# Two engines instead of one copy the transposed activations out of PSUM in a fused layernorm and linear kernel on eight cores

## The reference

```python
def reference(L0_attn_x, L0_ffn_weight, L0_ffn_bias, L0_ffn_kk, L0_ffn_aa):   # x: (1, 8192, 4096) f32
    def _L0_attn_ref(x):
        b, c, l = x.shape                       # b is 1
        q = jnp.transpose(x, (2, 0, 1))
        scale = jnp.asarray(c, x.dtype) ** 0.5
        scores = jnp.einsum('lnc,lmc->lnm', q, q) / scale
        prob = jax.nn.softmax(scores, axis=-1)
        msg = jnp.einsum('lnm,lmc->lnc', prob, q)
        return x + jnp.transpose(msg, (1, 2, 0))
    def _L0_ffn_ref(x, weight, bias, kk, aa):   # weight: (4096, 4096)
        w_b = aa * jnp.tanh(kk * weight)
        y = jnp.einsum('bsi,oi->bso', x, w_b)
        return y + bias
    x = L0_attn_x
    x = x + _L0_attn_ref(_layernorm(x, axis=-1))
    x = x + _L0_ffn_ref(_layernorm(x, axis=-1), L0_ffn_weight, L0_ffn_bias, L0_ffn_kk, L0_ffn_aa)
    return x
```

## Time and profile before

| | |
|---|---|
| median of 2 runs | 607.36 us (606.45 and 608.27) |
| the profiled execution | 604.37 us |
| its span on the slowest core, core 5 | 602.8 us |
| spans of the other cores | 592.7 to 600.9 us |
| TensorE busy | 498.2 us (83%) |
| ScalarE busy | 216.7 us (36%) |
| VectorE busy | 150.3 us (25%) |
| GpSimd busy | 83.6 us (14%) |

### The profile page before, as it was taken

One profiled execution on the slowest core, in us unless ns is written; L12 is line 12 of the kernel. 1 busy time (PEld: TensorE's weight loads), 2 busy tenths in 40 slices (PEclk: granted clock), 3 DMA queues, 4 the chain that ended last, 5 costly groups with the idle time before them and its releaser, 6 DMA issues.

```text
span 602.8 us, 7078 instructions; the slowest of 8 cores (592.7 to 602.8 us)
## 1 busy us (share of the span) xinstructions
PE 498.2 (83%) x2379; PEld 231.4 (38%) x2379; DVE 150.3 (25%) x336; ACT 216.7 (36%) x228; POOL 83.6 (14%) x118
## 2 busy tenths in 40 slices
PE   3034577556388999999999999998999899999993
PEld 3021133223244444444444444443444344444441
DVE  0800335632782120311032003200220023031120
ACT  0256577665544363036203722361036105500000
POOL 0001000020001120203030303030303031221111
PEclk9555676788598999999999999999899999999998
DMA  7959775369664599889988999999989999999543
GB/s 214 299 187 266 256 241 211 107 174 307 236 171 106 158 277 259 233 220 304 232 191 228 335 245 254 256 289 247 175 257 307 253 138 325 278 185 209 132 106 70
DMA packets 47699, 134.72 MB, mean 223 GB/s; under 512 B 5680, under 2 KB 5680, under 8 KB 46640
## 3 DMA queue, kind: packets, MB, share of 16 engines
q0 software_dynamic: 16416, 43.00, 35.0%
q1 hardware_dynamic: 20016, 50.37, 25.5%
q10 hardware_dynamic: 11232, 40.90, 21.4%
HBM read 117.47 MB, written 16.78 MB: 223 GB/s over the span
## 4 chain that ended last, share of the span: by engine, by line
DMA 41%; PE 35%; ACT 10%; issue 4%; DVE 4%; ACTq 3%; POOL 2%; SPq 1%; DVEq 1%; POOLq 0%
PE ps_acc L312 31%; DMA wring<-w2d 18%; DMA outs<-biasrow 12%; ACT wp L226 6%; DMA rb<-x 6%; DMA xs<-x 4%; PE ps_tr L289 3%; ACT h2T L246 2%; ACTq L229 1%; POOL outs L343 1%; ACTq L217 1%; ACT L235 1%; DVE outs L148 1%; DVE stats L160 1%; POOL wring L331 1%
## 5 line engine op out<-in xcount | busy, mean ns | idle before, releaser
L312 PE MATMUL ps_acc<-wp,h2T 128*128 128x512 bf16 x2048 | 461.0, 389 | 25.8 <-ACT wp L226 20.1
L312 PEld LDWEIGHTS ps_acc<-wp,h2T 128*128 128x128 bf16 x2048 | 203.6, 100 | 279.8 <-issue 49.7
L226 ACT ACTIVATE wp<-wring,kk_sb 128x1024 bf16<-128x1024 f32 x128 | 147.0, 1148 | 234.0 <-DMA wring<-w2d 171.2
L148 DVE SCALAR_TENSOR_TENSOR outs<-rb,s1a,ps_acc 128x512 f32<-128x512 f32 x64 | 47.7, 746 | 334.2 <-DMA rb<-x 211.9
L343 POOL DMA_DIRECT2D outs<-biasrow x64 | 56.4, 1069 | 262.8 <-DVE outs L152 250.8
L289 PE MATMUL ps_tr<-ident_sb,h2b 128*128 128x128 bf16 x256 | 30.9, 279 | 43.7 <-DVE h2b L196 30.5
L331 POOL DMA_DIRECT2D wring<-w2d x50 | 28.6, 606 | 250.2 <-ACT wp L226 229.3
L160 DVE BATCH_NORM_STATS2 stats<-xs 128x6 f32<-128x512 f32 x64 | 38.7, 679 | 27.0 <-DMA xs<-x 27.0
L289 PEld LDWEIGHTS ps_tr<-ident_sb,h2b 128*128 128x128 bf16 x256 | 20.8, 120 | 55.4 <-issue 52.4
L246 ACT CAST h2T<-ps_tr 128x512 bf16<-128x512 f32 x64 | 34.3, 584 | 18.1 <-PE ps_tr L289 17.5
L152 DVE TENSOR_SCALAR outs<-outs,b1a 128x512 f32<-128x512 f32 x64 | 32.2, 504 | 5.3 <-issue 0.4
(11 more groups left out here) (20 smaller groups left out, 24.3 us busy)
## 6 DMA issues: line engine op xcount, KB each, us to landing
wring<-w2d ACTq DMA_DIRECT2D x78, 512.0 KB, 7.2
wring<-w2d POOLq DMA_DIRECT2D x50, 512.0 KB, 6.8
xs<-x SPq DMA_DIRECT2D x8, 2048.0 KB, 11.7
rb<-x SPq DMA_DIRECT2D x64, 256.0 KB, 9.2
outs<-biasrow POOLq DMA_DIRECT2D x64, 256.0 KB, 9.3
y<-outs SPq DMA_DIRECT2D x64, 256.0 KB, 7.2
ident_sb<-ident SPq DMA_DIRECT2D x1, 32.0 KB, 3.1
kk_sb<-kk SPq DMA_DIRECT2D x1, 0.5 KB, 1.9
```

What stands on the lines that cost most here:

```text
L148: vector.scalar_tensor_tensor(outs[g % 4][:, :], rbb[g % 4][:, :], s1a[:, t:t + 1], ps_acc[g % 4][:, :], ALU.mult, ALU.add)
L226: scalar.activation(wp[ot % 2][:, jop * WPC:(jop + 1) * WPC], wr[:, sl * WPC:(sl + 1) * WPC], AF.Tanh, bias=0.0, scale=kk[:, :]).then_inc( ...
L312: mm = tensor.matmul(ps_acc[g % 4][:, :], h2T[:, t * D + ic * 128: t * D + (ic + 1) * 128], wp[ot % 2][:, ic * 512:(ic + 1) * 512], start= ...
```

## The change

The eight copies of a tile out of `ps_tr0` and `ps_tr1` are divided between two engines. ScalarE copies the even pieces (k = 0, 2, 4, 6), VectorE the odd ones (k = 1, 3, 5, 7). VectorE's copies count on a semaphore of their own, `s_evTo`, and TensorE waits on the one or the other by the parity of the piece. VectorE's four copies, each behind a wait for its transposed piece, stand after its two quarters of `h2b` and ahead of the evacuation and of the next tile's statistics. The function `issue_piece` on GpSimd is a rewriting that leaves its instructions as they are.

```diff
@@ vector
             vector.tensor_scalar(h2b[:, 1024:2048], xs[p][:, 1024:2048], sc[:, 6:7],
                                  sc[:, 7:8], ALU.mult, ALU.add).then_inc(s_v, 1)
+            for k in range(1, 8, 2):
+                vector.wait_ge(s_trT, 8 * t + k + 1)
+                vector.tensor_copy(h2T[:, t * D + k * 512: t * D + (k + 1) * 512],
+                                   ps_tr[1][:, :]).then_inc(s_evTo, 1)
             for g in evac_after_tile[t]:
                 emit_evac(g)
@@ scalar
-            for k in range(8):
+            for k in range(0, 8, 2):
                 scalar.wait_ge(s_trT, 8 * t + k + 1)
                 scalar.copy(h2T[:, t * D + k * 512: t * D + (k + 1) * 512],
-                            ps_tr[k % 2][:, :]).then_inc(s_evT, 1)
+                            ps_tr[0][:, :]).then_inc(s_evT, 1)
@@ tensor
                 if trg >= 2:
-                    tensor.wait_ge(s_evT, trg - 1)
+                    u = trg - 2
+                    tensor.wait_ge(s_evT if u % 2 == 0 else s_evTo, u // 2 + 1)
...
             if ot > 0:
-                tensor.wait_ge(s_evT, 8 * (t + 1))
+                tensor.wait_ge(s_evT, 4 * (t + 1))
+                tensor.wait_ge(s_evTo, 4 * (t + 1))
...
                 if ot == 0 and ic % 4 == 0:
-                    tensor.wait_ge(s_evT, 8 * t + ic // 4 + 1)
+                    k = ic // 4
+                    tensor.wait_ge(s_evT if k % 2 == 0 else s_evTo,
+                                   4 * t + k // 2 + 1)
```

More of the change, by code:

```diff
@@ L72, in build_nc @@
     s_evT = es.enter_context(sem("s_evT"))
+    s_evTo = es.enter_context(sem("s_evTo"))
     s_trT = es.enter_context(sem("s_trT"))
@@ L321, in _, with issue_piece @@
         gpsimd.wait_ge(s_xin[0], 16)
+        def issue_piece(w):
+            ot, j = divmod(w, NW)
+            sl = w % NWS
+            if w >= NWS:
+                gpsimd.wait_ge(s_wp, w - NWS + 1)
+            gpsimd.dma_start(wr[:, sl * WPC:(sl + 1) * WPC],
+                             w_h[ot * 128:(ot + 1) * 128,
+                                 j * WPC:(j + 1) * WPC]).then_inc(s_wl[sl], 16)
         def evens(ot):
@@ L325, in evens @@
                 w = ot * NW + j
[L326 to L333, removed]
+                if w % NWS >= 3:
+                    issue_piece(w)
         evens(0)
```

## The result

| | before | changed |
|---|---|---|
| median of all runs | 608.61 us (10 runs) | 623.5 us (11 runs) |
| ratio of the two kernels | | 1.0294, 95% interval 1.0235 to 1.0353 |
| profiled execution | 604.37 us | 618.02 us |
| spans by core in it | 592.7 to 602.8 us | 604.3 to 616.4 us |

The changed kernel is slower by 2.9%; the forecast was +9.1 us (1.5%) with a range up to 620. Runs in which one whole die was slowed, which both kernels have, are left out of the ratio and of all means and ratios that follow.

What follows compares the result with a forecast made beforehand. Up to group 7 the limits were a ScalarE loop, tile 5's load of x, then TensorE; afterwards TensorE at full clock. Loss 9.8 + 1.2 - 1.9 = +9.1 us on 607.36 gives 616.5 us, range 612 to 620.

Steps and rivals of the forecast that it cites:

- Part 1, the copies: Copies of transposed pieces from PSUM: dividing them gains close to nothing, since the loop through one buffer sets the period.
- The term of 0.1 us per tile: Odd buffer's loop, 0.12 us longer with VectorE's copy: two rounds at most 0.24 us, partly hidden, counted as 0.1 per tile.
- Part 2, ScalarE free earlier: Tiles 0 to 3: ScalarE's last copy ends 0.48 us earlier, a gain of 1.9 us in all.
- the rule of the step: Tiles 0 to 3: tanhs and square root start 0.48 us earlier, if VectorE has its statistics by then.
- the shift passes through the queues to tile 5's load: Tile 5's load of x, behind store, bias DMA, ring load and tile 3's first tanh, comes 1.9 us earlier; not certain.
- Part 3, VectorE held: Tiles 6 and 7: evacuation and statistics queue behind VectorE's last copy; each tile comes 17.8 us after the previous, losing 9.8 us.
- The sum: Whole kernel: 9.8 + 1.2 - 1.9 = +9.1 us, a median of 616.5 us.
- the lower end: Forecast's own range below: clock stays up -2.4, copy of 0.50 us -0.4, gain of 2.3 us; down to about 612.5.
- Everything after group 7 keeps its length: Groups 8 to 63: a block of fixed length at full clock; the kernel's end moves as much as group 7's end.
- The third rival: Part 2's gain misses tile 5 and group 7 runs wholly at 1.2 GHz: loss passes 2%, 12.1 us; 623.3 us; chance 0.24.
- The rival that the copies were the limit: ScalarE's 37 us of copies limit the kernel; halving them saves 18.7 us, giving 588.7 us; chance 0.03.
- VectorE's delay stays hidden: Group matmuls outlast VectorE's chain at tiles 6 and 7, so only part 2's gain is left: 605.5 us; chance 0.05.

Runs made afterwards that it cites:

- one moved copy: Against the kernel before, VectorE copies only the last piece (k = 7) in tiles 0 to 4, ScalarE all others; measured 0.9972 (0.9941 to 1.0003).
- four pieces moved in one block: Against the kernel before, VectorE copies the last four pieces in tiles 0 to 4, part of its other work ahead in tiles 1 to 3; 0.9833.
- The kernel that only waits: Against the kernel before, ScalarE keeps all eight copies; VectorE waits for each tile's last transposed piece before evacuation and next statistics; 1.0161, later 1.0167 and 1.0187.

## Why the prediction was right and wrong

**Part 1, the copies.** Right that they gain nothing. A copy on VectorE takes 0.691 us (0.70 taken). The term of 0.1 us per tile was too small: in tiles 1, 2, 3 and 5 the transposes took 5.86 us from first start to last end, and take 6.04 in the changed kernel, on every core. Of the two rounds of 0.12 us little is hidden. The last copy starts 6.14 us after the tile's first transposes (152.16, 158.30); the forecast's parts gave 6.03.

**Part 2, ScalarE free earlier.** Right in mechanism; the size was 1.13 us in tiles 1 to 4 instead of 3 x 0.48. Tiles 2 and 4 came 0.48 us closer, tile 3 only some 0.15 (19.45 us behind tile 2; 19.60 before, 19.11 with one moved copy). So the rule of the step holds, and the missing 0.3 us is VectorE's. In tile 3's tiny instructions it stands still for 0.42 us, waiting for nothing that the profile shows (core 0):

```profile
107.66 0.16 DVE L187 TENSOR_TENSOR sc<-sc 128x1 f32<-128x1 f32 x1
108.24 0.16 DVE L189 TENSOR_TENSOR sc<-sc,aa_sb 128x1 f32<-128x1 f32 x1 [0.42 <-issue]
```

The same stop, 0.39 to 0.43 us, is there on all eight cores; in tile 3 of the kernel before and of the one with one moved copy no core has it.

That the shift passes through the queues to tile 5's load can't be read from one profile: tile 4 to 5 varies from 21.8 to 27.1 us between cores of the changed kernel and from 22.2 to 30.4 of the kernel before. With four pieces moved in one block the shift is 8.0 us in tiles 1 to 4, tile 4 to 5 takes no longer than before (26.4 us against 27.4 and 25.2), and the mean core ends 11.0 us earlier, the upper end of the 6 to 11 expected. There the shift does pass.

**Part 3, VectorE held.** Right. Tile 5 to 7 became 36.0 instead of 25.8 us, +10.2 against 9.8 in the forecast. The 0.4 us more lie at tile 6 (18.17 us behind tile 5 against the forecast's 17.8), on whose way VectorE stops a second time, 0.43 us at L153; tile 7 followed after 17.8 as forecast. Tile 7 to the end of group 7 grew by 1.2 us on the six cores without the ceiling, as forecast, and by 1.4 to 1.5 in the later measurements. The kernel that only waits shows the cause.

**The sum** of +9.1 us came out near the loss of the mean core: +9.9, +9.4 and +9.5 us in the three later measurements (1.011 to 1.019). Part of that agreement may be luck. Against the one profile of the kernel before on these chips, the end of group 7 moved by only 6.0 to 6.3 us, because in that profile tile 1 began and tile 5's load landed late, and the second stage, for which the sum has nothing, grew by 4 to 5 us. One profile can't tell how much of this is the change. In the first pair of profiles, on the six cores without the ceiling, 8.7 us of the loss lie before the end of group 7 and 0.9 behind it. On the slowest core the loss was 11.7, 7.0 and 11.4 us: that core also waits longer for evacuations in the second stage, 18.0 us on core 2 in the second profile of the changed kernel. In the range, the lower end does not follow from its parts: 616.5 less 2.4, 0.4 and 0.4 is 613.3 and not 612.5.

**The step that failed** is the last one of the sum: "Everything after group 7 keeps its length", and with it the first sentences of the prediction, that from 195.5 us on TensorE runs at the full granted clock. In the first measurement pairs of cores did not: under a ceiling of 0.81 they ended 9.9 us later on the mean than the others (617.9 against 608.0), and in the profile 8 to 9 us of that is TensorE's own time behind group 7 (397.7 and 397.1 against 388.4 to 389.4). The metric takes the slowest core. Over the six runs it ends at 621.2 us on the mean; the slowest of the cores without the ceiling ends at 615.3, with which a run would take 616.9 (an estimate, on the low side, since only four to eight cores are left in each run), close to the forecast of 616.5. So some 6 us of the surplus are the ceiling's. It is not all: two of the six runs took 620.89 and 622.81 us though their slowest core was above 0.89, so the 1 us that the range adds for the spread of the medians was too little as well.

The third rival had the price (623.3 us) but not the mechanism: it put the low clock into group 7 alone and at its 1.2 GHz level throughout, after waits. What the trace shows began before tile 3, is a clock of 0.81, and ended at 265 us while TensorE was busy without a gap.

**Not settled.** Whether the change brings the ceiling. For it: in the first measurement five of six runs of the changed kernel have such pairs, while the profiled run of the kernel before (604.37 us) has none, and three of its ten runs (600.95, 605.37 and 605.55 us) are too short for one. That rests on an estimate: under the ceiling a core of the kernel before would end 10.6 us (608.0 less 597.4, the means of cores without it) ahead of one of the changed kernel, and runs would take 607 to 616 us. The other seven runs can be either, since their clocks are not on record. Against it: the nine runs of the changed kernel in three later measurements have none. It did not return, so no experiment could be made on it, and neither the divided copies nor the held queue are shown to be its cause. Whether the first measurement was on one of the three chips of the experiments is not on record.

The rival that the copies were the limit (588.7 us) is refuted by the kernel with copies divided in tiles 0 to 4: five eighths of its 18.7 us would have made 0.981, and 0.997 was measured, and the one that VectorE's delay stays hidden by the one that only waits.

## What to carry to other kernels

Before work is moved to an engine that is 25% busy, ask what stands behind it in that engine's queue and how early that work ran until now: here statistics that had run beside the transposes were put behind them, and 9.0 of the 10.2 us lost there came with a wait and no copy at all. What moved work gives back here is the time at which the busy engine is free, so give away the last pieces, not every second one, and fill the new engine's wait with what the next tile needs. Where each of eight cores can be the slowest, a forecast from one core's trace tends to come out low: the loss was 9.9 and 9.5 us on the mean core and 11.7 and 11.4 on the slowest in two of three measurements.

## What the runs showed that I had not expected

- The granted clock can have a ceiling between its two levels: on core 0, 0.81 where core 2 had 1.00, in the groups of tiles 3 to 7 and in the second stage until 265 us; 66 us of it held 248 matmuls instead of 299. It came in pairs of neighbouring cores, in one of four measurements of the same kernel.
- VectorE stops for about 0.4 us at fixed places of its program, for nothing that the profile shows: in the changed kernel 0.43 us at L153 in tile 5 and 0.39 to 0.43 at L189 in tile 3, on all eight cores. The kernel before has no stop over 0.3 us up to group 7. The one in tile 3 lies on the critical chain and cost the 0.3 us of part 2.
- A load of x was held by the order of SyncE's queue alone. Issued 15 us ahead of the store that used to precede it (108.58, 123.53), it took 8.2 us off the way from tile 4 to 5 and 7.9 off the mean core (597.0 to 589.1 us), although the edit moves that load and neither adds nor drops a transfer.
